# One fewer deferred scan block and a joint last half of W2 in a recurrent layer with a gated feed-forward branch, eight cores

## The reference

```python
xn = layernorm(x)                                   # over the 1024 features
# recurrent branch
Lambda = exp(-exp(nu_log) + 1j*exp(theta_log))
Bu = einsum('ph,blh->blp', (B_re + 1j*B_im)*gamma[:, None], xn)
xs = associative_scan(a_j*a_i, a_j*bu_i + bu_j)     # along the 8192 tokens
s  = einsum('hp,blp->blh', C_re + 1j*C_im, xs).real + D*xn
# feed-forward branch
h  = relu(xn @ W1 + b1)                             # 1024 -> 4096
g  = silu(h @ W2 + b2)                              # 4096 -> 1024
out = x + s*g
```

## Time and profile before

| | |
|---|---|
| median of 2 runs | 3748.74 us (3748.49 to 3749.0) |
| the profiled execution | 3751.26 us |
| its span, slowest core (6) | 3749.3 us |
| spans of the eight cores | 3706.2 to 3749.3 us |
| granted TensorE clock, mean of a core | 0.903 to 0.910 |
| TensorE matmul busy, core 6 | 3024.3 us (81%) |
| VectorE busy | 2196.8 us (59%) |
| ScalarE busy | 1114.7 us (30%) |
| DMA | 800.99 MB, mean 214 GB/s |
| chain that ended last, by engine | PE 48%, DVE 26%, DMA 15%, issue 6%, ACT 3% |

### The profile page before, as it was taken

The page is one execution under the profiler, slowest core; times in us unless marked ns, Lnnn a source line. Parts: engine busy times, 40 slices in busy tenths (PEclk is TensorE's granted clock), DMA queues, the critical chain, the costliest instruction groups (busy, mean ns, idle before and its releaser), DMA issues.

```text
span 3749.1 us, 62623 instructions; the slowest of 8 cores (3706.2 to 3749.3 us)
## 1 busy us (share of the span) xinstructions
PE 3024.3 (81%) x21760; PEld 2212.9 (59%) x21760; DVE 2196.8 (59%) x4122; ACT 1114.7 (30%) x2022; POOL 22.0 (1%) x46
## 2 busy tenths in 40 slices
PE   2401389898989898898988888998989898988998
PEld 1200258485766657484856667584857666574867
DVE  5681057474756757474747667474747567574501
ACT  3201332332333232323322232323323332323222
POOL 0010000000000000000000000000000000000000
PEclk9855599898999999998989999999989999998999
DMA  5776549395766758394966668494957667593866
GB/s 141 175 171 147 152 145 289 130 299 171 262 220 215 248 179 293 132 296 135 295 200 225 225 201 276 145 290 140 298 180 249 214 221 261 170 295 133 283 231 215
DMA packets 409237, 800.99 MB, mean 214 GB/s; under 512 B 50528, under 2 KB 50528, under 8 KB 406880
## 3 DMA queue, kind: packets, MB, share of 16 engines
q1 hardware_dynamic: 361184, 738.26, 61.0%
q10 hardware_dynamic: 41984, 41.95, 3.2%
q0 software_dynamic: 5760, 16.78, 3.0%
HBM read 755.01 MB, written 58.72 MB: 217 GB/s over the span
## 4 chain that ended last, share of the span: by engine, by line
PE 48%; DVE 26%; DMA 15%; issue 6%; ACT 3%; DVEq 1%; ACTq 0%; SPq 0%; POOL 0%; POOLq 0%
PE PB L564 12%; PE PB L786 11%; PE PB L696 6%; PE PA L829 6%; PE PA L696 6%; PE PB L829 5%; DMA wslot<-sc_w 4%; DMA wslot<-sc_b 4%; DVE s_b L860 3%; DMA h<-W 3%; DVE sS L212 3%; DVE cS L209 3%; DVE tmp L205 2%; DVE tmp L207 2%; DMA sc_w<-h 2%
## 5 line engine op out<-in xcount | busy, mean ns | idle before, releaser
L786 PE MATMUL PB<-xnf,wslot 128*128 128x256 bf16 x8192 | 934.1, 278 | 42.5 <-DMA wslot<-sc_w 41.8
L786 PEld LDWEIGHTS PB<-xnf,wslot 128*128 128x128 bf16 x8192 | 817.2, 100 | 158.7 <-issue 47.0
L796 ACT ACTIVATE h<-PB,b_tab 128x256 bf16<-128x256 f32 x1024 | 485.7, 474 | 584.4 <-PE PB L786 539.3
L829 PE MATMUL PA<-h,wslot 128*128 128x256 bf16 x4096 | 468.0, 273 | 44.2 <-ACT h L796 42.6
L829 PE MATMUL PB<-h,wslot 128*128 128x256 bf16 x4096 | 468.1, 273 | 0.0
L829 PEld LDWEIGHTS PA<-h,wslot 128*128 128x128 bf16 x4096 | 398.4, 98 | 98.1 <-issue 52.3
L829 PEld LDWEIGHTS PB<-h,wslot 128*128 128x128 bf16 x4096 | 400.9, 98 | 46.3
L696 PE MATMUL PB<-xnf,wslot 128*128 128x512 bf16 x1024 | 258.2, 416 | 84.2 <-DMA wslot<-sc_b 84.2
L860 DVE SCALAR_TENSOR_TENSOR s_b<-xnf,d_tab,s_b 128x256 f32<-128x256 bf16 x256 | 124.1, 485 | 336.9 <-ACT g_b L843 311.7
L426 PE MATMUL PB<-ident,s_b 128*128 128x128 f32 x256 | 62.1, 424 | 305.5 <-ACT s_b L418 213.1
L719 DVE TENSOR_TENSOR xsre<-vv,cS 128x512 bf16<-128x512 bf16 x128 | 88.6, 692 | 369.9 <-ACT vv L707 357.9
(11 more groups left out here) (89 smaller groups left out, 2667.0 us busy)
## 6 DMA issues: line engine op xcount, KB each, us to landing
wslot<-sc_w SPq DMA_DIRECT2D x256, 2048.0 KB, 11.1
wslot<-sc_b SPq DMA_DIRECT2D x32, 2048.0 KB, 10.2
wslot<-sc_c SPq DMA_DIRECT2D x32, 2048.0 KB, 10.5
xsl<-x SPq DMA_DIRECT2D x32, 1024.0 KB, 5.9
out<-xsl ACTq DMA_DIRECT2D x32, 1024.0 KB, 4.4
h<-W POOLq DMA_DIRECT2D x8, 1024.0 KB, 14.5
sc_w<-h SPq DMA_DIRECT2D x8, 1024.0 KB, 8.4
h<-W POOLq DMA_DIRECT2D x32, 256.0 KB, 4.4
```

Of the source, the lines that this page charges most:

```text
L786: inst = nc.tensor.matmul(bank[:, 0:256], pslot(jw)[:, kk * 1024 + ml * 128: kk * 1024 + (ml + 1) * 128], xnf_p[:, kk * NSUP + sub * NSUB: ...
L796: ev = S(lambda m2=mi, b=bank: nc.scalar.activation(h1[:, m2 * NSUB:(m2 + 1) * NSUB], b[:, 0:256], AF.Relu, bias=b1_tab[:, m2:m2 + 1]))
L829: inst = nc.tensor.matmul(w2bank[m], pslot(jw)[:, kl * 1024 + m * 128: kl * 1024 + (m + 1) * 128], h1[:, (q * 8 + kl) * NSUB: (q * 8 + kl ...
```

## The change

In the loop over m of the B product, `emit_rest(m - 2)` now runs for m = 2 to 7, so rest 5 comes behind the rotation of chunk 7, and only rests 6 and 7 are deferred. In W2, quarters 0 and 1 stay as they were. Quarters 2 and 3 become one phase: TensorE waits for both pieces, then goes through the output chunks m, doing the 8 matmuls of quarter 2 and the 8 of quarter 3 for each; chunk m is complete after its 16 matmuls, and its Silu follows. Both pieces get their `piece_done` at the end of that phase.

```diff
-                if 2 <= m <= 6:
+                if m >= 2:
                     emit_rest(m - 2)
             if not has_prev:
-                for mm2 in range(5, CH):
-                    emit_rest(mm2)
+                emit_rest(CH - 2)
+                emit_rest(CH - 1)
...
-                for q in range(4):
+                for q in range(2):
                     jw = w2p[sub][q]
                     pump()
                     piece_wait(jw)
...
+                jw2, jw3 = w2p[sub][2], w2p[sub][3]
+                pump()
+                piece_wait(jw2)
+                piece_wait(jw3)
+                gm2 = 0
+                for m in range(CH):
+                    inst = None
+                    for q, jw in ((2, jw2), (3, jw3)):
+                        for kl in range(CH):
+                            inst = nc.tensor.matmul(
+                                w2bank[m],
+                                pslot(jw)[:, kl * 1024 + m * 128:
+                                          kl * 1024 + (m + 1) * 128],
+                                h1[:, (q * 8 + kl) * NSUB:
+                                   (q * 8 + kl + 1) * NSUB],
+                                start=False,
                                 stop=(q == 3 and kl == CH - 1),
                                 skip_group_check=True)
...
+                    gm2 = TE.inc(inst)
+                    SX(TE, gm2)
+                    new_gev[sub][m] = S(
+                        lambda bnk=w2bank[m], mm=m:
+                        nc.scalar.activation(
+                            g_b[:, mm * NSUB:(mm + 1) * NSUB], bnk,
+                            AF.Silu, bias=b2_tab[:, mm:mm + 1]))
+                piece_done(jw2, gm2)
+                piece_done(jw3, gm2)
...
                 if sub == 0 and has_cur:
-                    for mm2 in range(5, CH):
-                        emit_rest_deferred(mm2)
+                    emit_rest_deferred(CH - 2)
+                    emit_rest_deferred(CH - 1)
```

More of the change, by code:

```diff
@@ L823, in build_program @@
                     inst = None
-                    gm = 0
                     for m in range(CH):
@@ L835, in build_program @@
                                 start=(q == 0 and kl == 0),
+                                stop=False, skip_group_check=True)
+                    gm = TE.inc(inst)
+                    piece_done(jw, gm)
+                jw2, jw3 = w2p[sub][2], w2p[sub][3]
[14 more added lines that the diff above has]
+                                start=False,
                                 stop=(q == 3 and kl == CH - 1),
                                 skip_group_check=True)
[L838 to L848, removed]
+                    gm2 = TE.inc(inst)
[7 more added lines that the diff above has]
+                piece_done(jw3, gm2)
                 for jj, b in enumerate(ppb):
```

## The result

The changed kernel is slower: the ratio to the kernel before is 1.0558, 95% interval 1.0513 to 1.0602. Its profiled execution took 3968.36 us against 3751.26 before, 217 more. The forecast was 3807 (range 3755 to 3880), within 2%. The mechanism was that of rival 1, but the size lay beyond it (3880), and beyond the worst case of the bounds too (3934).

What follows compares the result with a forecast made beforehand. TensorE was taken to set the pace, but interrupted by waits. The terms 102 + 18 + 5 - 35 - 21 - 14 + 3 = +58 us on 3751.3 gave 3809, or 3807 as the median; range 3755 to 3880.

Steps and rivals of the forecast that it cites:

- rival 1: W2's joint phase: waits as long as the trace's loads, clock drops at each; +131, so 3880 us; chance 0.37.
- worst case of the bounds: Whole kernel: every term at its unfavourable bound, without the rivals; +185 us, 3934.
- wait for q3: W2's joint phase: quarter 3 needed one quarter earlier, landing 10.2, wait 3.2 us in 32 phases; +102 (64 to 138).
- lower clock behind it: Matmuls behind the joint phase's wait: a long wait, about one in three, costs 1.67 us more; +18 (0 to 53).
- gap before the C product: Behind `sub` 1's W2: wait for C_im instead of VectorE, start 9.7 us after W2, not 12.05; -35 (-57 to -15).
- gap behind `sub` 0, with the moved rest: Behind `sub` 0's W2: earlier Silus save 1.3 us per iteration, -21; the rest in the B loop costs +3.
- W1 of `sub` 1: wait before its quarter 3: W1 of `sub` 1: quarter 3's load queues behind later-released loads, +0.3 us per iteration; +5 (0 to 16).
- W1 of `sub` 1: clock behind the gap: Start of W1 in `sub` 1: one shorter idle time keeps the clock higher, 0.9 us per iteration; -14 (-27 to 0).
- C, transposes, B, W1 of `sub` 0: The other stages of the iteration: no term in the forecast's sum, 0 us.
- The moved rest: Rest 5 in the B loop before `sub` 0's Silus: nearly covered by quarter 3's wait; 0.2 x 16 = +3 us.
- rival 3: End of `sub` 0: with a shorter quarter 3 wait the moved rest holds back the Silus; +25, 3774 us; chance 0.06.
- The rule on DMA time: Quarter 3's load: 2.0 us plus bytes over 436 GB/s gives 6.8 us for 2 MB, making the +102 0.

Runs made afterwards that it cites:

- e3: The kernel before with one added wait: TensorE waits for W2's quarter 3 already before quarter 2; ratio 1.0253, 3845 us.
- e6: The kernel before, with TensorE waiting for W2's quarter 3 before quarter 2 and quarter 2's slot released at quarter 3's end; ratio 1.0565.
- e4: The kernel before, with the slot of W2's quarter 2 released only at the end of quarter 3, together with quarter 3's; ratio 1.0061.
- e5: The changed kernel with only the first half (1 MB) of W2's quarter 3 loaded, all matmuls kept; ratio 1.0145.
- f2: The changed kernel (rest moved, joint phase) with weight pieces of 1 MB in six slots; ratio 0.9733, 3649 us.
- f1: The kernel before with weight pieces of 1 MB in six slots, same SBUF, bytes and order of matmuls; ratio 0.9749, 3654 us.
- f6: The kernel before with 1 MB pieces in six slots, four W2 quarters, and half of `emit_rot` moved into the C product; spans 3597 to 3621 us.

## Why the prediction was wrong

The mechanisms that the prediction named came out; their sizes did not: every term came out less favourable than forecast. The terms of the sum, in us over the whole kernel. The measured column is from the waits, the two halves of the joint phase and the stages. The forecast's term for W1 of `sub` 1 is split into its two parts.

| term | predicted | measured |
|---|---|---|
| wait for q3 | +102 | +130 (130.2) |
| lower clock behind it | +18 | +56 (285.2 - 228.8) |
| gap before the C product | -35 | -11 (15 x (11.37 - 12.09)) |
| gap behind `sub` 0, with the moved rest | -18 | -16 (16 x (5.91 - 6.88)) |
| W1 of `sub` 1: wait before its quarter 3 | +5 | +33 (16 x (1.59 + 0.50)) |
| W1 of `sub` 1: clock behind the gap | -14 | -8 (16 x (7.97 - 8.44)) |
| C, transposes, B, W1 of `sub` 0 | 0 | +27 (15 x 1.79) |
| sum | +58 | +211 of 217 |

The step that failed worst is the clock term, "Of today's landings about one in three would give a wait as long as that": 30 of 32 waits paid, 38 us more than forecast. Four others were mis-sized by 24 to 28 us each: the landing of q3, the landing of C_im, the "+0.3 per iteration" for W1's quarter 3, and the other stages, which the sum put at nothing without a reason.

**The wait for q3.** Mechanism and place were right, and the early wait and the shorter load show it. I took 10.2 us for the landing, below the trace's mean of 10.6, because I expected thinner traffic. In the changed kernel the 32 loads landed after 9.7 to 13.2 us, 10.8 in the mean, and TensorE began 6.98 + 4.07 = 11.05 after quarter 0's end, so some 0.2 us more pass around the load. The discount was a guess with no row behind it, and by the mean of the rows the term would have been +115.

**The clock.** The sentence took the length of the wait as the cause, from two rows. In the changed kernel the clock fell behind 30 of the 32 waits, also the short ones, and cost 1.3 to 2.9 us each time. TensorE's timeline and the granted clock (third last column) of one:

```profile
2811.94 8.81 PE L847 MATMUL PA<-h,wslot 128*128 128x256 bf16 x64 [3.00 <-DMA wslot<-sc_w]
...
2811.90:2813.90 2.00, 1.96 (x11) 1.45 (x12) 1.69 (x4) 0.00 (x0) 0.00 (x0) 0.60 1.05 410
```

The wait was 3.00, less than the 3.38 that cost nothing in the earlier trace rows, and the 64 matmuls took 8.81 instead of 7.15. Before W1's quarter 1 in the same execution a wait of 3.69 cost nothing, and one of 3.09 cost 2.8. In the joint phase itself two waits cost nothing, 3.46 and 3.49 long, neither among the shortest:

```profile
2100.94 21.12 PE L786 MATMUL PB<-xnf,wslot 128*128 128x256 bf16 x192 [3.69 <-DMA wslot<-sc_w]
...
2547.05 23.96 PE L786 MATMUL PB<-xnf,wslot 128*128 128x256 bf16 x192 [3.09 <-DMA wslot<-sc_w]
...
3104.06 7.15 PE L847 MATMUL PA<-h,wslot 128*128 128x256 bf16 x64 [3.46 <-DMA wslot<-sc_w]
```

So neither the length of a wait near 3 us nor its place decides alone, and what does is open. The upper bound of +53 was nearly the right value. The rule cited in the prediction ("TensorE: Matmul & The Clock Gate", "HAM oscillation — how this bites in real kernels", in the Trainium skill) spoke for it: by it the drop is paid at every wait. The trace agrees for 30 of the 32 here, and not for most waits before W1's quarter 1.

**The gap before the C product.** That C_im would take VectorE's place was right. Its landing was not: the product could start 9.7 us after W2's end by the forecast, and the landing of C_im by itself took 10.9 in the mean. The forecast leaned on one pair of loads in another place, where the kernel before had 15 landings of C_im itself with a mean of 10.7. Two thirds of the saving was gone. This term also made the cost of the early wait final: e3 got a part of the wait back in that gap, e6 and the change did not. The prediction's sum priced wait and release as separate terms; e3, e4 and e6 show that 0.0253 + 0.0061 becomes 0.0565.

**W1 of `sub` 1.** The place that the prediction named came out: behind the pair of loads, quarter 3 of W1 is late. It was put at 0.3 us per iteration, and in 13 of 14 iterations TensorE waited for it, 1.59 us in the mean, with 0.50 of slow matmuls behind the wait:

```profile
2163.27 21.12 PE L786 MATMUL PB<-xnf,wslot 128*128 128x256 bf16 x192
2187.76 8.76 PE L786 MATMUL PB<-xnf,wslot 128*128 128x256 bf16 x64 [3.36 <-DMA wslot<-sc_w]
```

The clock behind the gap was kept up better, as predicted: the first quarter of W1 took 7.97 us in the mean against 8.44 (in the iteration shown, the full clock), half of the 0.9 that I had counted. e4, which has only the late release, waits in the same place, 1.3 us in the mean, and grew by the same 1.6.

**The other stages.** I put nothing there. The C and B products have no wait inside them and took 0.66 and 0.50 us longer, so at a lower clock; the C product's first 32 matmuls, behind the longer idle time, account for 0.44. W1 of `sub` 0 waits 3.2 instead of 2.6 us for its quarter 1, and the matmuls behind it took 0.5 longer.

**The moved rest.** Nearly covered, as predicted, in the change; worth 0.9% alone, with +0.7 and -6.0 us in the two sub-blocks where up to +2.8 and some -5 were expected; and the hold on the Silus of rival 3 came out in e5 and f2.

**The rule on DMA time.** The estimate of 6.8 us for 2 MB ("DMA: Bandwidth & Descriptors", "Anatomy of one DMA — SWDGE (gpsimd) path", in the Trainium skill) does not hold for these loads with eight cores at work: 10.8 in the mean in the joint phases. The section's fit is for loads that GpSimd issues, and these are issued on SyncE's queue. The measurement decides.

## What to carry to other kernels

When two stages that each consume a prefetched buffer are merged, count in units of the buffer ring: the last piece is needed one slot-time earlier and the first is released one slot-time later. Price both together, because a wait that other engines' backlog would have paid back is not paid back if the late release delays the next stage's weights. Pieces of half the size in twice as many slots give the same SBUF a finer release; here this alone was worth 2.5%, and with it the merged phase no longer cost anything. To take the price of a load, use the rows of that same load in the same place where the trace has them.

## What the runs showed of the hardware

- Loads of 2 MB, eight cores at work: C_im took 9.7 to 11.9 us when issued with another load at the end of W2, and 9.5 to 11.9 alone in the kernel before; the first of a pair at the end of the B product took 8.7 in the earlier trace rows. The same form of load has no one latency.
- Loads of 1 MB with runs of 1 KB (f1) carried the same bytes without a wait for weights in the iterations, so the shorter runs did no harm that TensorE noticed. The DMA engines were busy for longer, 6% more in all: the queue's packets took 66.6% of a span of 3648 us instead of 61.0% of 3749. First the kernel before, then f1:

```profile
q1 hardware_dynamic: 361184, 738.26, 61.0%
```

```profile
q1 hardware_dynamic: 693984, 738.28, 66.6%
```

- A wait of 3.00 us was followed by a stretch with a mean granted clock of 0.60, while one of 3.69 elsewhere left the next 192 matmuls at 21.12 us, the time of the full clock.
- In f6 the granted clock was 0.81 for some 15 us in the middle of W1 of `sub` 1, with TensorE busy before and throughout. Idle time is not the only thing ahead of a lower clock.
